# Scan stage: one of eight drive products on VectorE instead of GpSimd

## What is computed

```python
def step(state, inp):
    d, b, c, u = inp
    dA = jnp.exp(d[..., None] * A)
    state = state * dA + (d * u)[..., None] * b[:, None, :]
    y = jnp.einsum('bdn,bn->bd', state, c)
    return (state, y)
...
_, ys = jax.lax.scan(step, state0, (dt_t, B_t, C_t, u_t))
```

## Time and profile before

| | us |
|---|---|
| median of 3 runs | 1661.8 |
| range of the runs | 1660.62 to 1667.61 |
| the profiled execution | 1659.59 |
| its span in the profile | 1657.0 |
| busy: TensorE, VectorE, ScalarE, GpSimd | 1433.2, 1312.2, 1043.7, 1247.6 |
| GpSimd: drives (L1237), 128 | 313.2 |
| GpSimd: multiplies by C (L1254), 128 | 311.1 |
| GpSimd: adds into y (L1260), 128 | 307.5 |
| VectorE: scans (L1151), 256 | 310.8 |

### The profile page before, as it was taken

The page is one execution under the profiler, slowest core; times in us unless marked ns, Lnnn a source line. Parts: engine busy times, 40 slices in busy tenths (PEclk is TensorE's granted clock), DMA queues, the critical chain, the costliest instruction groups (busy, mean ns, idle before and its releaser), DMA issues.

```text
span 1657.0 us, 23284 instructions
## 1 busy us (share of the span) xinstructions
PE 1433.2 (86%) x7632; PEld 1150.1 (69%) x7632; DVE 1312.2 (79%) x2375; ACT 1043.7 (63%) x2407; POOL 1247.6 (75%) x613
## 2 busy tenths in 40 slices
PE   4555689999989999989999999997478999898996
PEld 1113578878868878868877878876265687676784
DVE  3996588899888899888899888887547768487575
ACT  3995366666656666656666656665347757577474
POOL 1344199999899999999999899999557448166263
PEclk9766889999999999999999999998588999899998
DMA  4466614434623433633443632424342122122021
GB/s 164 166 218 223 204 57 128 136 93 141 226 74 125 136 115 128 223 102 109 128 150 100 215 112 86 125 73 142 119 131 86 33 97 66 38 89 70 27 71 58
DMA packets 122817, 198.23 MB, mean 120 GB/s; under 512 B 10868, under 2 KB 60536, under 8 KB 121160
## 3 DMA queue, kind: packets, MB, share of 16 engines
q1 hardware_dynamic: 122696, 196.75, 37.0%
HBM read 150.18 MB, written 46.53 MB: 119 GB/s over the span
## 4 chain that ended last, share of the span: by engine, by line
PE 37%; DVE 23%; POOL 17%; issue 13%; ACT 6%; DMA 2%; SPq 1%; POOLq 0%; DVEq 0%; ACTq 0%
PE banks L589 9%; PE banks L590 8%; PE banks L591 8%; POOL act_buf L1908 5%; POOL state L1237 4%; POOL state L1254 4%; DVE state L1151 4%; PE banks L1452 2%; PE banks L1454 2%; PE banks L1453 2%; DVE banks L443 2%; DVE banks L414 1%; DVE ow_lo L1060 1%; DVE banks L1966 1%; DVE w_lo L1055 1%
## 5 line engine op out<-in xcount | busy, mean ns | idle before, releaser
L1254 POOL TENSOR_TENSOR state<-state,Cn 128x1024 f32<-128x1024 f32 x128 | 311.1, 2430 | 52.9 <-DVE state L1151 52.6
L1260 POOL TENSOR_TENSOR y_sb<-y_sb,state 128x1024 f32<-128x1024 f32 x128 | 307.5, 2402 | 21.5 <-DMA y_sb<-scratch_y 11.1
L1151 DVE TENSOR_TENSOR_SCAN state<-banks,state 128x512 f32<-128x512 f32 x256 | 310.8, 1214 | 3.4 <-ACT banks L973 2.2
L1237 POOL TENSOR_TENSOR state<-dtu_sb,Bn 128x1024 f32<-128x1024 f32 x128 | 313.2, 2448 | 0.1
L1908 POOL TENSOR_TENSOR act_buf<-act_buf,wb 128x512 f32<-128x512 f32 x128 | 165.4, 1294 | 171.4 <-ACT act_buf L1808 169.6
L973 ACT ACTIVATE banks<-dt_sb,negA 128x512 f32<-128x512 f32 x256 | 177.4, 693 | 116.8 <-DVE state L1151 115.9
L589 PE MATMUL banks<-x_hi,w_hi 128*128 128x512 f32 (+1 forms) x512 | 189.2, 369 | 38.4 <-DVE qT_lo L1081 25.2
L591 PE MATMUL banks<-x_hi,w_lo 128*128 128x512 f32 (+1 forms) x512 | 178.7, 349 | 0.0
L590 PE MATMUL banks<-x_lo,w_hi 128*128 128x512 f32 (+1 forms) x512 | 178.6, 349 | 0.0
L589 PEld LDWEIGHTS banks<-x_hi,w_hi 128*128 128x128 f32 x512 | 101.8, 199 | 58.8 <-DVE qT_lo L1081 30.7
L1956 DVE TENSOR_TENSOR hid_lo<-banks,hid_hi 128x512 fp32r<-128x512 f32 x136 | 93.8, 689 | 54.5 <-ACT hid_hi L1820 52.5
(11 more groups left out here) (217 smaller groups left out, 4440.7 us busy)
## 6 DMA issues: line engine op xcount, KB each, us to landing
x_hi<-scratch_xs SPq DMA_DIRECT2D x32, 512.0 KB, 4.8
x_lo<-scratch_xs SPq DMA_DIRECT2D x32, 512.0 KB, 6.0
Bn<-scratch_bc SPq DMA_DIRECT2D x64, 256.0 KB, 4.0
Cn<-scratch_bc SPq DMA_DIRECT2D x64, 256.0 KB, 3.4
scratch_acc<-acc_sb SPq DMA_DIRECT2D x64, 256.0 KB, 2.1
wb<-scratch_wT SPq DMA_DIRECT2D x64, 256.0 KB, 3.2
acc_sb<-scratch_acc SPq DMA_DIRECT2D x48, 256.0 KB, 3.0
w_stage<-in_w SPq DMA_DIRECT2D x32, 256.0 KB, 3.6
```

What stands on the lines that cost most here:

```text
L1151: nc.vector.tensor_tensor_scan(row, dA[:, :], row, 0.0, ALU.mult, ALU.add) \
L1237: nc.gpsimd.tensor_tensor(st[:, k % 4], dtu[:, 2 * h:2 * h + 2, :], Bn[:, state % NB, :].unsqueeze(1).broadcast_to([P, 2, T]), ALU.mult).t ...
L1254: nc.gpsimd.tensor_tensor(st[:, k % 4], st[:, k % 4], Cn[:, state % NB, :].unsqueeze(1).broadcast_to([P, 2, T]), ALU.mult).then_inc(S["gat ...
L1260: nc.gpsimd.tensor_tensor(y[:, 2 * h:2 * h + 2, :], y[:, 2 * h:2 * h + 2, :], st[:, k % 4], ALU.add).then_inc(S["piece_done"], 1)
```

## The change

Every eighth drive, k % 8 == 5, moves to VectorE: the second half of the state of each round with p % 4 == 2. That is 16 of 128. VectorE makes it right behind scan 4p of that round, ahead of the combine. It has a semaphore of its own, `dbu_vector`, and the waits of SyncE and of the scans count the two semaphores apart.

```diff
+def by_vector(k):
+    return k % 8 == 5
+
+
+def vector_drives(n):
+    return (n + 2) // 8
+
+
+def pool_drives(n):
+    return n - vector_drives(n)
...
             if p + 2 < NSTATE:
-                sp.wait_ge(S["dbu_done"], 2 * p + 2)
+                sp.wait_ge(S["dbu_done"], pool_drives(2 * p + 2))
+                if by_vector(2 * p + 1):
+                    sp.wait_ge(S["dbu_vector"], vector_drives(2 * p + 2))
                 load_b(sp, p + 2)
...
+        def drive(k):
+
+            state = k // 2
+            dve.wait_ge(S[f"b_loaded{state % NB}"], 16 * (state // NB + 1))
+            dve.wait_ge(S["piece_done"], k - 3)
+            nc.vector.tensor_tensor(st[:, k % 4], dtu[:, 2:4, :],
+                                    Bn[:, state % NB, :].unsqueeze(1).broadcast_to([P, 2, T]),
+                                    ALU.mult).then_inc(S["dbu_vector"], 1)
+
         def scan(i):
             dve.wait_ge(S["dA_done"], i + 1)
-            dve.wait_ge(S["dbu_done"], i // 2 + 1)
+            if by_vector(i // 2):
+                dve.wait_ge(S["dbu_vector"], vector_drives(i // 2 + 1))
+            else:
+                dve.wait_ge(S["dbu_done"], pool_drives(i // 2 + 1))
...
             if p < NM:
                 scan(4 * p)
+                if by_vector(2 * p + 1):
+                    drive(2 * p + 1)
                 combine(2 * p)
...
-            if k + 3 < NDRIVE:
+            if k + 3 < NDRIVE and not by_vector(k + 3):
                 drive(k + 3)
```

More of the change, by code:

```diff
@@ L580, in attend_and_scan @@
              "b_loaded0", "b_loaded1", "c_loaded0", "c_loaded1",
-             "dA_done", "dbu_done", "scan_done", "gated", "piece_done")
+             "dA_done", "dbu_done", "dbu_vector", "scan_done", "gated", "piece_done")
     S = {n: ctx.enter_context(nc.semaphore(n)) for n in names}
@@ L724, in sync @@
             if r == NS - 1 and b + 1 < B:
-                sp.wait_ge(S["dbu_done"], 2 * NS * (b + 1))
+                sp.wait_ge(S["dbu_done"], pool_drives(2 * NS * (b + 1)))
+                sp.wait_ge(S["dbu_vector"], vector_drives(2 * NS * (b + 1)))
                 load_half(sp, dtu, "dtu", b + 1, 1)
@@ L740, in sync @@
             if r == NS - 2 and b + 1 < B:
-                sp.wait_ge(S["dbu_done"], 2 * NS * (b + 1) - 1)
+                sp.wait_ge(S["dbu_done"], pool_drives(2 * NS * (b + 1) - 1))
                 load_half(sp, dtu, "dtu", b + 1, 0)
```

## The result

| | before | after |
|---|---|---|
| median of 4 runs each, us | 1661.21 | 1688.95 |
| range of the runs | 1660.33 to 1667.61 | 1684.97 to 1693.64 |
| ratio, with its 95% interval | | 1.0163 [1.0141, 1.0185] |
| the profiled execution | 1659.59 | 1689.63 |
| its span in the profile | 1657.0 | 1687.8 |

The changed kernel is slower by 27.7 us. The forecast was 1678, slower by 16, with a range of 1663 to 1691: side and range hold, and the size is missed by 11 us. The narrower 1670 to 1686, which the prediction gave for its forecast alone, is missed too.

What follows compares the result with a forecast made beforehand. TensorE was taken to set the pace in plain rounds, VectorE where weights are split, not GpSimd. Terms 4 + 6 + 5 + 0 + 1 = 16 us on the median gave 1678 us, range 1663 to 1691.

Steps and rivals of the forecast that it cites:

- GpSimd is not the bound: Fused stage: GpSimd full but not late; relief gives back only 0.6 us. The opposing rival, 1640 us, had chance 0.05.
- the form waits: VectorE's product with a broadcast operand waits for the running GpSimd instruction, costing from 1.13 to about 3.5 us.
- The rival that it costs only itself: Products on VectorE never wait for GpSimd and cost 1.13 us each: +4, 1666 us; chance 0.2.
- round 58: Pattern for rounds without weights: product waits 1.75 us for GpSimd's add, ends 2.9 late; TensorE loses 0.8 us.
- rounds 10, 26, 42: Middle of the weights: product 1.5 us, 0.9 after idle time, plus about 1 for the split: 2 each, 6 us.
- The 1 us for the split behind it: Rounds 10, 26, 42: the weight split behind the product meets a lengthened GpSimd instruction, about 1 us more.
- the relief, put at nothing: Sixteen products off GpSimd, some 38 us of busy time, give back only 0.6 us; the gain becomes waits for scans.
- rounds 14, 30, 46: Last weights: product about 2.4 us, less 0.6 to 0.8 of idle time: 1.7 each, 5 us.
- rounds 2, 18, 34, 50: Output weights: VectorE's 2.05 us idle absorbs most of the product; 0, with 2 us each way per round.
- the end: Round 62, where VectorE bounds the last rounds: 1.7 us lost, 0.6 won, +1.
- The clock rival: Longer TensorE stalls in weight rounds bring seven clock falls, +11 on top of 16: 1689 us; chance 0.15.
- the plain rounds: Rounds 6, 22, 38, 54, 58, without weights: TensorE loses 0.8 us in each, 4 us together.

Runs made afterwards that it cites:

- the products left out: Changed kernel with the 16 moved products made by neither engine, scans running over what is in the buffer: 1663.4 us, 1.0006 of the kernel before.
- the product made twice: Kernel before, GpSimd making all 128 products, with VectorE repeating the 16 behind scan 4p: 1695.8 us, 1.0222.
- the kernel with six products: Changed kernel with VectorE making only the products of rounds 10, 14, 26, 30, 42 and 46: 1688.0 us, 1.0148 of the kernel before.
- A maximum with one operand: Kernel before with an unused maximum over half of dtu on VectorE at each of the 16 products' places: 1679.8 us, 1.0124.
- two maxima: Kernel before with two unused maxima of 1.19 us each on VectorE in rounds 10, 14, 26, 30, 42 and 46 only: 1680.4 us, 1.0105.

## Why the prediction was right or wrong

**Right: GpSimd is not the bound.** Its busy share spoke for it, its waits against it, and the run with the products left out says 1.0006. The chain, which the prediction puts on GpSimd's side, gave it 17% of the span, less than TensorE (37%) and VectorE (23%). But the prediction took it that relief comes to nothing more than longer waits. It also moves the starts of GpSimd's instructions, and that is not free in every round.

**Right: the form waits.** The product with a broadcast operand, of which the trace of before has no row, takes 2.2 to 3.25 us in the stage where the earlier trace rows has 1.22. The rival that it costs only itself (1666) is out in the changed kernel. That this was the likely side came from the rows on the splits; the Trainium skill, SBUF — State Buffer, section Who interferes with whom, names every VectorE instruction with two inputs in SBUF, and the trace agrees: 16 of 16 products waited behind scan 4p.

**Right: round 58.** Phase, 2.9 us, 3.38 on GpSimd's next instruction and the new wait of TensorE for the heads all came as drawn. The term was 0.8 a round and measured 0.5: 2.6 us in five rounds instead of 4.

**Wrong in size: rounds 10, 26, 42.** Forecast 6, measured 11.2, and 13.7 with the rounds around them. The step that failed is "GpSimd is nearer to a boundary here, so I take 1.5 us for the product": it measured 3.24. Near a boundary the value is either 1.2 to 1.5 or 3.2 to 3.4, not something between, and it hangs on a few tenths of a microsecond. The earlier trace rows tell where the split stands, not where the product would. The trace of before has the row that tells it, and the prediction doesn't use it:

```profile
588.11 2.39 POOL L1260 TENSOR_TENSOR y_sb<-y_sb,state 128x1024 f32<-128x1024 f32 x1
```

The scan at 587.09 is followed at 588.22, 0.11 us behind the start of this add. So the boundary had just been passed, and a product there pays for a whole GpSimd instruction, whether GpSimd is relieved (0.22 us behind a start, 3.24 us) or not (0.10 and 3.37, the product made twice). The 1 us for the split behind it was wrong as well: that split took 0.68.

The second step that failed is the relief, put at nothing. With the products left out these twelve rounds grow by 6.4 us: 3.9 in rounds 10, 26 and 42, by their second splits, and 2.5 in the others. If the two simply add, which no run shows, the product's own share is 13.7 - 6.4 = 7.3 us, 2.4 a round, against the forecast 6.

**Wrong in size: rounds 14, 30, 46.** Forecast 5, measured 8.3 with the rounds behind them. The product took 3.24 to 3.25 us, where I had 2.4, and costs the round 2.4, 2.3 and 2.5 us, where I had 1.7 after subtracting idle time; that is 7.2. Rounds 13, 29 and 45 grow by 2.2, which the kernel with the products left out shows as well (+1.18, +0.56, +0.50): relief again. The clock takes 1.3 in round 14, and a fall that the trace of before had in round 46 is gone, 2.4.

**Right to a microsecond: rounds 2, 18, 34, 50 (0, measured -1.5) and the end (+1, measured +1.9).** For the first that is luck as much as judgement: single rounds among 17 to 18, 33 to 34 and 49 to 50 lie between -4.4 and +4.7 us in the experiments. The end is luck in part too: with the products left out it is 1.9 us shorter than before, so the product costs more than forecast there and the relief gives more back.

**The clock rival.** Its 1689 is the time that was measured, and that is chance. It wanted seven more falls at 1.6 us on top of the 16. The falls that can be priced add 1.3 us (round 14) and take away 2.4 (round 46); another, in round 42, costs nothing (17.17 us at 0.90, as rounds 10 and 26 at 1.00). The mean granted clock, 0.926 where it was 0.929, stands for some 7 us more of TensorE's clock lost over the whole span, but a loss while TensorE waits costs nothing, so this is no price. As a mechanism the fall exists, up to 2.4 us each in rounds 14, 30 and 46; it came and went in both kernels and is no part of the price that can be shown. In the output-weight rounds that stays open.

The terms were short by 9.1 us in the stage: 7.7 in rounds 9 to 12 and repeats, 3.3 in 13 to 16 and repeats, 0.9 at the end, less 1.4 in the plain rounds and 1.5 in those with output weights (rounded). The other 2.6 us, from 25.1 to the median's 27.7, can't be placed: the 25.1 is from one profile of each kernel, and their runs spread over 7 and 9 us. Between the two profiles what lies outside the stage is mostly the start, and that differs from run to run.

**What stays open.** What makes the clock fall in round 14, 30 or 46 of one kernel and not of the next, and the changes of a few microseconds in the output-weight rounds, I could not take apart: the splits there wait in other phases and the clock falls by other amounts, both at once. The median of the kernel with six products is 26.3 above the kernel before, 6 more than its stage; its start, 6.4 us later in the profile, would cover that, but one profile doesn't show it for the median.

## What to carry to other kernels

An engine that is busy for 59.37 of 60 us is not the bound while nobody waits for it: read who waits, and if it is no one, work taken off it turns into waiting, and into other starts of what is left. Where two engines hold each other up, as VectorE and GpSimd do here, a new or delayed instruction can cost a whole instruction of the other engine or nothing, so look up not only where it lands but where everything behind it lands, against the start of the other engine's next instruction, and expect the relief itself to move those starts. The same 16 products cost 27.7 us in one place and 8.7 in the next; try the place where the other engine is waiting first.

## What the runs showed of the hardware

- The multiply with a broadcast second operand waits for a running GpSimd instruction like the splits do: 1.19 to 1.20 us when it finds GpSimd idle (10 times), 1.40 to 3.38 when not. A maximum with one operand never waited (1185 to 1193 ns, 16 times, each in the midst of a GpSimd instruction).
- VectorE never waited for more than one GpSimd instruction, also where GpSimd runs without a gap. It gets in at the next boundary, and GpSimd's following instruction takes 3.2 to 3.4 us instead of 2.39 where it meets such a product. The wait and the lengthening are inside the durations; no wait row shows them.
- One fall of TensorE's granted clock cost 1.3 to 2.4 us where it fell into round 14, 30 or 46, next to nothing (0.1) where it ended just ahead of round 30, and 0.0 in rounds 10, 26 and 42, where TensorE waits for the heads longer (2.8 us); beside the delay of two maxima it cost nothing in round 30 either.
- Rounds without a change and without splits of weights repeat within 0.1 us between kernels and chips, so differences round by round resolve costs that the median of the whole cannot.
